# A kernel of a state-space layer and a routed low-rank projection: the set-up is written anew, with four peeled steps

## The reference, cut to what is computed

```python
dt = exp(log_dt); A = -exp(log_A_real) + 1j * A_imag; dtA = A * dt[:, None]
Cs = Cc * (exp(dtA) - 1.0) / A
K = 2.0 * einsum('hn,hnl->hl', Cs, exp(dtA[:, :, None] * arange(1024))).real
mask = arange(1024) < length[:, None]
y = irfft(rfft(x * mask, 2048) * rfft(K, 2048))[..., :1024] + x * mask * D[:, None]
x = x + y * mask
logits = x @ Wr.T + 5.0 * one_hot(language)
topw, topi = top_k(logits, 2)                    # softmax over the two: gates
lora = einsum('bter,bte,eor->bto', x @ A, gates, B)
out = x + x @ W.T + 2.0 * lora
```

## Time and profile before

| | us |
|---|---|
| median of 3 runs | 696.15 (695.85 to 696.51) |
| the profiled execution | 695.72 |
| its span, first to last instruction | 693.9 |

### The profile page before, as it was taken

One profiled execution on the slowest core, in us unless ns is written; L12 is line 12 of the kernel. 1 busy time (PEld: TensorE's weight loads), 2 busy tenths in 40 slices (PEclk: granted clock), 3 DMA queues, 4 the chain that ended last, 5 costly groups with the idle time before them and its releaser, 6 DMA issues.

```text
span 693.9 us, 12598 instructions
## 1 busy us (share of the span) xinstructions
PE 645.8 (93%) x3621; PEld 615.2 (89%) x3621; DVE 490.0 (71%) x1531; ACT 467.8 (67%) x973; POOL 20.4 (3%) x46
## 2 busy tenths in 40 slices
PE   3364999999999999999999999999999999999997
PEld 2353899999999999999999999999999999999997
DVE  8876567777776767777776767777776767777621
ACT  4784577677768677677768677777768677675411
POOL 2000000000000000000000000000000000000000
PEclk9875899999999999999999999999999999999999
DMA  7123023222123233223123233223123223221112
GB/s 241 49 69 89 11 68 70 54 52 68 32 67 68 68 68 68 53 53 68 31 68 68 68 68 68 53 53 68 31 68 68 68 68 68 53 53 39 31 32 60
DMA packets 22869, 43.36 MB, mean 62 GB/s; under 512 B 8104, under 2 KB 13512, under 8 KB 22856
## 3 DMA queue, kind: packets, MB, share of 16 engines
q1 hardware_dynamic: 17576, 26.42, 17.1%
q10 hardware_dynamic: 5280, 16.78, 9.5%
HBM read 26.35 MB, written 16.84 MB: 62 GB/s over the span
## 4 chain that ended last, share of the span: by engine, by line
DVE 36%; ACT 25%; issue 18%; PE 13%; ACTq 6%; DMA 2%; DVEq 1%; SPq 0%
DVE state L783 17%; PE pmg L1104 9%; ACTq L470 5%; ACT result L488 4%; ACT u_hi L416 4%; ACT turn L379 3%; ACT L393 3%; DVE y_lo L830 3%; ACT swapped L439 2%; ACT Z L405 2%; DVE Z L770 2%; ACT xt L413 2%; DVE c_lo L764 2%; ACT z_swap L398 2%; PE pc L1029 2%
## 5 line engine op out<-in xcount | busy, mean ns | idle before, releaser
L1104 PE MATMUL pmg<-w_hi,y_hi 128*128 128x388 f32 (+1 forms) x768 | 268.7, 350 | 1.7 <-ACT result L488 0.2
L1104 PE MATMUL pmg<-w_hi,y_lo 128*128 128x388 f32 (+1 forms) x768 | 260.1, 339 | 0.0
L1104 PE MATMUL pmg<-w_lo,y_hi 128*128 128x388 f32 (+1 forms) x768 | 259.8, 338 | 0.0
L1104 PEld LDWEIGHTS pmg<-w_hi,y_hi 128*128 128x128 f32 x768 | 144.3, 188 | 7.5 <-ACT result L488 6.5
L1104 PEld LDWEIGHTS pmg<-w_hi,y_lo 128*128 128x128 f32 x768 | 144.6, 188 | 0.2
L1104 PEld LDWEIGHTS pmg<-w_lo,y_hi 128*128 128x128 f32 x768 | 144.2, 188 | 0.0
L439 ACT ACTIVATE swapped<-state 64x128 f32<-64x128 f32 x192 | 59.3, 309 | 67.1 <-DVE state L783 65.7
L783 DVE SCALAR_TENSOR_TENSOR state<-swapped,scan_tab,state 128x192 f32<-128x192 f32 (+1 forms) x240 | 73.8, 349 | 12.1 <-ACT swapped L439 0.2
L812 DVE TENSOR_TENSOR s_lo<-state,s_hi 128x896 fp32r<-128x896 f32 x32 | 35.0, 1093 | 31.5 <-ACT s_hi L461 31.5
L744 DVE TENSOR_TENSOR u_lo<-xt,u_hi 128x1024 fp32r<-128x1024 f32 x32 | 39.2, 1225 | 24.8 <-ACT u_hi L416 24.8
L461 ACT ACTIVATE s_hi<-state 128x896 fp32r<-128x896 f32 x32 | 30.5, 953 | 35.0 <-DVE state L783 35.0
(11 more groups left out here) (195 smaller groups left out, 1068.1 us busy)
## 6 DMA issues: line engine op xcount, KB each, us to landing
rows<-in_x SPq DMA_DIRECT2D x64, 256.0 KB, 5.1
out<-result ACTq DMA_DIRECT2D x62, 256.0 KB, 3.0
toe<-kpad SPq DMA_DIRECT2D x32, 128.0 KB, 4.5
result<-in_L_cond_W SPq DMA_DIRECT2D x5, 512.0 KB, 7.2
rows<-in_L_cond_W SPq DMA_DIRECT2D x2, 512.0 KB, 7.8
result<-in_L_cond_A SPq DMA_DIRECT2D x1, 512.0 KB, 5.8
b_rows<-in_L_cond_B SPq DMA_DIRECT2D x1, 512.0 KB, 7.0
xt<-in_L_cond_W SPq DMA_DIRECT2D x1, 512.0 KB, 8.8
```

What stands on the lines that cost most here:

```text
L1104: ins = nc.tensor.matmul(pm[:, n, 0:c1 - c0], y[s][:, c, :], w[:, c, c0:c1], start=(c == 0 and y is y_hi and w is w_hi), stop=(c == CH - 1 ...
```

## The change

What it does, engine by engine:

- VectorE no longer works out the decay exponential; ScalarE does, with its own exponential. The first group's turns and the far-chunk turns are made earlier in the list.
- The kernels of pairs 0 and 1 are made as rows: a product of a 0/1 matrix `pick` with Z2 on TensorE, a copy `k_row` on ScalarE, and a store and Toeplitz load through `kpad_rows`. Z2 of group 0 is made in two halves.
- W tiles have more room: `w0_rows` is a buffer of its own, `b_sorted` holds W4 until B needs it, `px` is a third PSUM place for turning. The tiles' order is new, B is last and sorted by ScalarE.
- The banks of pair 0 begin when y of pair 0 and the first tiles are there; the other tiles are turned between parts of them. Steps (0,0) and (0,1) are written out; steps (1,0) and (1,1) are the function `step` with `early=True`: the convolution of the next pair stands after the first bank, and the routing before the merge. The loop starts at 2.
- SP loads the rows of pair i+4 instead of i+3 ahead of the kernel's store.

```diff
-        w_rows = [xt1_rows, rows[0][:, :], result[0][:, :], result[1][:, :], result[0][:, :], result[1][:, :],
-                  rows[1][:, :], result[1][:, :]]
-        a_rows = result[0][:, :]
...
+        w_rows = [w0_rows[:, :], rows[0][:, :], result[0][:, :], result[1][:, :],
+                  b_sorted[:, :, :, :].rearrange("p o e r -> p (o e r)"), result[0][:, :], rows[1][:, :], result[1][:, :]]
+        a_rows = result[0][:, :]
...
-        TILE = [(A_, in_pm, 0), (B_, in_pc, 0), (W_, in_pm, 6), (W_, in_pc, 0), (WR_, in_pm2, 0), (W_, in_pm, 7),
-                (W_, in_pc, 1), (W_, in_pm, 2), (W_, in_pc, 3), (W_, in_pm, 4), (W_, in_pc, 5)]
+        TILE = [(A_, in_pm, 0), (W_, in_pc, 6), (W_, in_pm, 7), (WR_, in_pm2, 0), (W_, in_pm, 0), (W_, in_px, 2),
+                (W_, in_pc, 1), (W_, in_pm, 3), (W_, in_px, 4), (W_, in_pc, 5), (B_, in_pc, 0)]
...
+            sp.wait_ge(tables, 3)
+            sp.dma_start(bass.AP(kpad.tensor, 2 * P, [[2 * KPITCH, PAIRS], [1, 2]]), k_first[:, :]).then_inc(pad_stored, 16)
+            with nc.allow_non_contiguous_dma(reason="four samples"):
+                sp.dma_start(bass.AP(kpad_rows.tensor, P, [[KPITCH, DUO], [1, 1]]), k_first[0:DUO, :]
+                             ).then_inc(pad_stored, 16)
+            store_row(0)
+            sp.wait_ge(pad_stored, 64)
+            load_toe_rows(0)
+            store_row(1)
+            load_toe_rows(1)
+            load_w(4)
+            sp.dma_start(b_rows[:, :, :, :].rearrange("p e o r -> p e (o r)"),
+                         B.rearrange("e (p o) r -> p e (o r)", o=8)).then_inc(b_in, 16)
             sp.wait_ge(wt_full, w_tile(7) + 1)
             load_w(3)
+            sp.wait_ge(px_full, 2)
+            load_rows(0, 3)
+            sp.wait_ge(wt_full, w_tile(2) + 1)
+            load_w(5)
             sp.wait_ge(wt_full, w_tile(1) + 1)
             load_rows(0, 2)
-            sp.wait_ge(wt_full, w_tile(2) + 1)
-            load_w(4)
             store_kernel(0, 2)
             load_toe(0, 2)
-            sp.wait_ge(wt_full, w_tile(3) + 1)
-            load_w(5)
...
+            def turn_first_powers(j):
+
+                for h in (2 * j, 2 * j + 1):
+                    ins = nc.scalar.activation(Z2[:, h, :], Z[:, h, :], ACT.Copy, scale=gen_scalar(C2_RE, 0, h, False))
+                ins.then_inc((z_half, z_swapped)[j], 1)
+
+            def kernel_row(j):
+                act.wait_ge(row_full, j + 1)
+                nc.scalar.activation(k_row[j][:, :], row_psum[:, j, :], ACT.Copy).then_inc(k_ready, 1)
+
+            def sort_b():
+                act.wait_ge(b_in, 16)
+                act.wait_ge(wt_full, w_tile(4) + 1)
+                nc.scalar.activation(b_sorted[:, :, :, :].rearrange("p o e r -> p e o r"), b_rows[:, :, :, :], ACT.Copy
+                                     ).then_inc(b_ready, 1)
...
+            act.wait_ge(par_dve, DT_STEPS)
+            nc.scalar.activation(expo, dt_re, ACT.Exp).then_inc(par_act, 1)
             nc.scalar.activation(tanh_half, dt_re, ACT.Tanh, scale=0.5).then_inc(par_act, 1)
             copy_parameters(0, 1)
             act.wait_ge(consts, 3)
...
-            swap_odd(0, 0, 2)
-            waves(1)
-            split_obs(0, 0, first=True)
-            split_toe(0, 0, first=True)
-            split_states(0, 0, first=True)
+            split_rows(0, 1, first=True)
             weight(3)
-            split_rows(0, 1, first=True)
             split_obs(0, 1, first=True)
-            magnitudes(1, False, reused=True)
+            split_y(0, 0)
             weight(4)
             weight(5)
-            split_y(0, 0)
+            weight(6)
+            magnitudes(1, False, reused=True)
+            weight(7)
+            ratios(0, 0)
+            weight(8)
+            swap_powers(1)
+            sort_b()
+            weight(9)
+            turn_powers(1, False)
+            weight(10)
             copy_states(0, 1)
-            swap_powers(1)
-            turn_powers(1, False)
             swap_odd(0, 1, 0)
-            split_toe(0, 1)
+            split_gated(0, 0)
             swap_odd(0, 1, 1)
-            weight(6)
             swap_odd(0, 1, 2)
+            split_toe(0, 1, toe_rows_back)
+            split_states(0, 1)
+            finish(0, 0)
+            split_rows(0, 2)
             split_ctr(0, 2)
-            split_states(0, 1)
             split_obs(0, 2)
-            for k in range(7, WTILES):
-                weight(k)
-            split_rows(0, 2)
-
-            def step(b, m, rows_left=True, ahead=True, kernels=True):
+            split_y(0, 1)
+            copy_states(0, 2)
+            act.wait_ge(gen_staged, 1)
+            turns_of(None, True)
+            swap_odd(0, 2, 0)
+            magnitudes(None, True)
+            swap_odd(0, 2, 1)
+            swap_odd(0, 2, 2)
+            split_toe(0, 2)
+            split_states(0, 2)
+            split_ctr(0, 3)
+            split_obs(0, 3)
+            waves(2)
+            split_rows(0, 3)
+            swap_powers(2)
+            turn_powers(2, True)
+            nc.scalar.activation(warm[:, :], phase[:, 0:1], ACT.Exp)
+            ratios(0, 1)
+            split_y(0, 2)
+            split_ctr(0, 4)
+            split_gated(0, 1)
+            copy_states(0, 3)
+            swap_odd(0, 3, 0)
+            finish(0, 1)
+            split_obs(0, 4)
+            swap_odd(0, 3, 1)
+            split_toe(0, 3)
+            swap_odd(0, 3, 2)
+            split_states(0, 3)
+            split_rows(0, 4)
+
+            def step(b, m, rows_left=True, ahead=True, kernels=True, early=False):
                 if kernels and m == 0:
                     act.wait_ge(gen_staged, b + 1)
                     turns_of(None, True)
                 if kernels and m == 1:
                     swap_powers(b + 2)
                     turn_powers(b + 2, True)
+                if early and kernels and m == 1:
+                    nc.scalar.activation(warm[:, :], phase[:, 0:1], ACT.Exp)
+                if early:
+                    ratios(b, m)
                 split_y(b, m + 1)
                 if kernels and m == 0:
                     magnitudes(None, True)
-                if kernels and m == 1:
+                if not early and kernels and m == 1:
                     nc.scalar.activation(warm[:, :], phase[:, 0:1], ACT.Exp)
-                ratios(b, m)
+                if not early:
+                    ratios(b, m)
                 if rows_left:
                     copy_states(b, m + 2)
...
+                                     op0=ALU.add, op1=ALU.add).then_inc(tables, 1)
+            split_rows(0, 0)
+            rotate_first_powers(0)
+            split_ctr(0, 0, kernel=False)
+            rotate_first_powers(1)
+            low_weight(0)
...
             low_weight(3)
+            split_obs(0, 1)
+            dve.wait_ge(masks, 4)
+            merge(0, 0)
             split_rows(0, 1)
-            split_obs(0, 1)
+            split_y(0, 0)
             low_weight(4)
             low_weight(5)
-            dve.wait_ge(masks, 4)
-            merge(0, 0)
+            low_weight(6)
             powers(1)
-            split_y(0, 0)
+            low_weight(7)
+            route(0, 0)
+            low_weight(8)
+            low_weight(9)
+            rotate_powers(1, False)
+            low_weight(10)
             scanning = scan_states(0, 1, staged=False)
             next(scanning)
-            rotate_powers(1, False)
-            next(scanning)
-            low_weight(6)
-            next(scanning)
+            next(scanning)
+            split_gated(0, 0)
+            next(scanning)
+            next(scanning)
+            split_toe(0, 1, toe_rows_back)
+            split_states(0, 1)
+            split_rows(0, 2)
             split_ctr(0, 2)
-            next(scanning)
-            split_toe(0, 1)
-            split_states(0, 1)
             split_obs(0, 2)
-            for k in range(7, WTILES):
-                low_weight(k)
-            split_rows(0, 2)
-
-            def step(b, m, rows_left=True, ahead=True, kernels=True):
+            merge(0, 1)
+            split_y(0, 1)
+            angles(2)
+            dve.wait_ge(scan_staged, 1)
+            scanning = scan_states(0, 2)
+            next(scanning)
+            next(scanning)
+            next(scanning)
+            next(scanning)
+            split_toe(0, 2)
+            split_states(0, 2)
+            split_ctr(0, 3)
+            split_obs(0, 3)
+            split_rows(0, 3)
+            powers(2)
+            rotate_powers(2, True)
+            route(0, 1)
+            merge(0, 2)
+            split_y(0, 2)
+            split_ctr(0, 4)
+            split_gated(0, 1)
+            scanning = scan_states(0, 3)
+            next(scanning)
+            split_obs(0, 4)
+            next(scanning)
+            split_toe(0, 3)
+            next(scanning)
+            next(scanning)
+            split_states(0, 3)
+            split_rows(0, 4)
+
```

(75 more changed lines are left out.)

324 lines of the change are left out of this document (174 added, 150 removed).

## The result

The changed kernel takes 711.28 us, the median of 4 runs (710.09 to 711.99), where the kernel before takes 696.33 in the same comparison (695.85 to 697.55): a ratio of 1.021, 95% interval 1.019 to 1.023, or 15.0 us more. The forecast was 709.7, in a range of 698 to 716.

A forecast was written before the change was run, and what follows sets the result against it. TensorE mostly waits before 77 us and is full after; its 15 us early lead is lost waiting for ScalarE and VectorE, pair 5's first bank slips from 174.45 to 188.5: 695.7 + 14 = 709.7 us, range 698 to 716.

The forecast's parts named there:

- y(0): y of pair 0, after set-up: complete at 43 to 44.5 us instead of 48.85, with its banks beginning there.
- W: W tile loads in the set-up: W4 asked for at about 32 us, W5 at 42 and there at 49 to 50.
- The rival of late W tiles: W3, W4 or W5 come so late that pair 0's banks stand still (W5 after 51): 712 to 716 us; chance 0.06.
- Parameters: Set-up: about 2 us of VectorE exponential steps go, yet powers come only 0.1 us sooner, C2 the same: nothing gained.
- Kernel rows: First kernels made as rows in set-up: 0.3 us per product or copy, 0.3 to 1.3 in all, 0.6 given back; net 0.
- y(1): y of pair 1, fed by ScalarE and VectorE: complete at 79.5 to 80.5 us, only 1 us sooner.
- c_lo(4): Low part of pair 4's controllability table, which pair 1's gates need: at 107 us, 27 us behind y(1).
- Idles about 10 of the 27: TensorE between y(1) and c_lo(4): 14.5 us of work before pair 1's gates, so about 10 of 27 us idle.
- zo behind the result copies: ScalarE's queue: pair 4's zo stands behind pair 1's result copies and stores, leaving VectorE idle 5 to 6 us.
- y(3): y of pair 3: complete at 131.5 to 132.5 us; pair 3's first bank then at 145 instead of about 135.5.
- The rival that the chain keeps up: ScalarE and VectorE deliver c_lo(4) by 95 us, so the 15 us lead stays: 684 us (681 to 690); chance 0.14.
- The rule weighed in the prediction: Turned tiles between pair 0's first banks would keep TensorE's clock low: 4 us more there, the sum unchanged.

The follow-up runs named there:

- e4: The changed kernel with the decay exponential back on VectorE as 14 steps between the parameter steps: 711.49 us.
- e1: The changed kernel with steps (1,0) and (1,1) back in the loop's order on TensorE, ScalarE and VectorE: 707.10 us.
- e5: The changed kernel with the three engines' lists reordered from the parameters' second transpose to the end of step (1,1), two warm-up exponentials left out: 672.54 us.

## Why the prediction was right

Step by step, by the signs that it named:

- y(0): 42.76 + 1.23 = 43.99 (43 to 44.5 forecast), the first bank 44.09.
- W: the toe of pair 0 is issued at 23.77 us (25 forecast), W5 at 42.68 (42) and turned at 50.56, when by the median landing of 7.7 us behind the issue it has only just come (an estimate: 50.4). B's sorting took 1.06 us (1.0 to 2.0). The rival of late W tiles had 51 as its point of decision and missed it by half a us.
- Parameters: mis-sized. "Powers 0.1 us sooner" was 0.7 (14.31 against 15.03). e4 shows the part under it: 1.9 us from the exponential, of which the moved far-chunk steps take 1.2. By e4 even the 1.9 us change nothing that the times resolve, so the miss was harmless. I had seen that the Sin table comes no sooner (10.88 against 10.82) and took it for the end of the chain, which it wasn't.
- Kernel rows: four products took 1.01 us in all and a copy 0.25, where 0.3 was taken for each. Their net of 0 wasn't tried.
- y(1): 80.18 (79.5 to 80.5). The idle times of TensorE ahead of it: 3.31 at rows 2, 3.53 at control 2, 1.43 and more at y(1), forecast 3, 4, 2 to 3.
- c_lo(4): 106.67 + 0.42 = 107.09 (107). Gates' wait 3.88 (3 to 6). "Idles about 10 of the 27" doesn't follow from its own terms: 27 less 14.5 of work is 12.5. Measured are 8.3 us idle and 18.7 busy from 80 to 107 us, since part of the products ran at half clock (0.75 in the mean). The sum doesn't hang on it, as c_lo(4) comes from the other engines.
- zo behind the result copies: VectorE idle 6.73 us (5 to 6), copies and stores at 113.9 to 117.2.
- y(3): 132.03 + 1.23 = 133.26 (131.5 to 132.5), pair 3's first bank 146.16 (145), pair 6's powers 157.31 (155 to 157), pair 4 171.06 (168.6 to 170.5), pair 5 190.19 (187.6 to 189.5). The forecast was 1 to 2 us too low here, the size of the 1.6 us by which the time is over it. A wait that my working didn't name lies in this stretch: in step (1,1) the route stands ahead of merge 4, and VectorE waits in it for pair 3's first bank, which TensorE begins late, at 146.16:

```profile
152.20 0.17 DVE L932 TENSOR_TENSOR logits<-pmg,bias 128x8 f32<-128x8 f32 x1 [5.72 <-PE pmg L1221]
```

  In e1, where the route is behind the merge again, this wait is gone (no idle time ahead of the logits of pair 3 at 153.17). Pair 3's first bank is no sooner there (146.95), but pair 4's is 5.0 sooner (166.09 against 171.06), so the gain of e1 arises in this stretch; that it is the route's alone isn't shown. I had counted the early routes as work, not as a wait.
- The loop's step is as before, but it is 19.5 us and not the 19.2 of the forecast: ten steps lie between the stores at 331.49 and 526.66 us before (195.2 us) and between those at 308.19 and 503.57 in the changed kernel (195.4). The 38.3 us of two steps in the earlier trace rows were too short a stretch. TensorE is 99% busy (99.18 of 100 us from 200 to 300; before 99.08).

The number owes little to luck: the signs came out one by one along the path that was forecast, and the misses in the sum are of 1 to 2 us.

The rival that the chain keeps up (684 us) had its condition right. It asked that the queues between y(1) and c_lo(4) shrink from 27 to 15 us, and so they nearly do in e5, where y(1) is complete at 68.19 and c_lo(4) at 84.95, 16.8 us, by a better order alone. Its argument "even at their best these engines need 15.5 us a step" was no obstacle.

TensorE's clock: the half-clock stretches were where the forecast put them (0.75 in 80 to 107, 0.82 in 107 to 132, 0.94 in 132 to 160, 1.00 from there), and a part of their cost falls into waits. Another part does not. Behind the late gates of pair 1 the rows of pair 4 are turned at half clock, in 1.94 us where it was 1.03 for pair 3's, and the last bank, for which the result copies wait, is behind them (110.39 us, against 89.65).

In the changed kernel convolution 0 runs at half clock, then three W tiles are turned with no products between them but two small ones by the identity for each tile (clock of 38 to 40, 40 to 41, 41 to 44 and 44 to 46 us):

```profile
38.00:40.00 2.00, 2.00 (x7) 1.67 (x6) 1.27 (x3) 0.71 (x3) 0.00 (x0) 0.50 0.63 141
40.00:41.00 1.00, 1.00 (x8) 1.00 (x7) 0.77 (x3) 0.00 (x0) 0.00 (x0) 0.64 0.06 20
41.00:44.00 3.00, 2.75 (x26) 2.56 (x23) 2.98 (x5) 2.33 (x3) 0.00 (x0) 1.00 0.13 33
44.00:46.00 2.00, 1.91 (x12) 1.91 (x13) 2.00 (x2) 1.98 (x3) 0.00 (x0) 1.00 0.87 274
```

The clock rises from 1.2 to 2.4 GHz while transposes run, stays there while two more tiles are turned, and the banks with turned tiles between them begin at full clock. The rise itself may be owed to the convolution's twelve products right ahead of the first tile; in the kernel before, 4 us of transposes and small identity products alone (69.85 to 73.95 us) stand ahead of the rise, and the clock is 0.90 from 74.6 to 75.0, with the convolution's first products. The rule weighed in the prediction (the Trainium skill, "TensorE: Matmul & The Clock Gate", section "Part 4: PE-mode transpose": no full clock for transposes) doesn't agree with these traces, which show 1.00 while tiles are turned; the 4 us that the prediction put on it were not to be seen.

## What to carry to other kernels

An engine that is ahead has gained nothing until the ones that feed it are: ask of each step in the new place which queue it must come through, and what stands in front of it there that it doesn't need. Where engines hand each other small pieces and none is full, write the lists so that two or three pairs' work alternates, keep copies that wait for the busiest engine behind those that others wait for, and find the order by adding up durations of rows; here that gave every experiment's time to within 4 us, and the same work in another order went from 15 us slower than before to 26 us faster. Doubling a piece of work in two places is a cheap way to see on which of them the chain lies, if it is large beside the spread of the times; 2.7 us were barely enough here.

## What was not expected of the hardware

- The issue of two stores on ScalarE took 1.12 to 1.25 us nearly everywhere, up to 1.76 in places and 3.83 once. That of pair 5's two loads on SP took 1.2 in one kernel and 3.06 and 3.48 in two others, each time at about 80 us, and later pairs' took 2.45 and 2.90 in two more. It costs the issuing engine that time, and what stands behind it.
- The eight transposes of a W tile took 1.44 us while the clock was rising and 1.04 behind it, 0.13 us each; in the kernel before, at half clock, they took 1.94.
